# An eight-stage transformer stack on one core: stacked head operands issued inside later stages, a buffer of its own for head sums, sparse operands padded to 128 rows, and one first-layer operand made on ScalarE

## The chip, the core and the metric

The kernel runs on one core of a Trainium2 chip. The metric is device time in microseconds (us) of one execution. TensorE is called PE below, VectorE DVE, ScalarE ACT, GpSimd POOL, and SyncE (which only issues DMAs here) SP.

## The reference, cut to what matters

`x` is (1, 2048, 128), float32. Eight blocks follow each other, each added to `x` after a layernorm:

```
x = x + L0_attn(ln(x))   # windowed "bond" attention, 16 heads of 8, window 64
x = x + L0_ffn(ln(x));  x = x + L1_attn(ln(x));  x = x + L1_ffn(ln(x))
x = x + L2_attn(ln(x))   # dense attention fused with a top-k sparse attention
x = x + L2_ffn(ln(x));  x = x + L3_attn(ln(x));  x = x + L3_ffn(ln(x))
```

The parts that the change touches:

```
# L0_attn, for each head, query t and each of the 64 keys before it
strain = disp_win - disp
damage = sigmoid(gelu(strain @ W_dmg + b_dmg) @ W_dmg_out + b_dmg_out)
logits = gelu(strain @ W_strain + rel_emb @ W_pos) @ W_bond - 10 * damage

# L2_attn: 16 heads of 8, s = 2048, R = 64, kk = 409
dense  = softmax(q k^T / sqrt(8)) v  @ out_proj + b          # per head
QK     = (src Qp + bq) @ (src Kp + bk)^T / sqrt(64)           # 2048 x 2048, inner size 64
aw     = softmax(QK); keep the kk largest of each row, renormalise; sparse = aw @ V
x      = layernorm(src + sig(lam) * dense + (1 - sig(lam)) * sparse); ff; layernorm
# L3_attn: 16 heads of 8, plain softmax attention with scales
```

## The kernel before, in words

The kernel is written as a sequence of blocks. In a block each engine runs its own list; a block ends only when all five lists have ended (SP's too), and the next block starts then. Inside a block the order on an engine is the order in which the code issues, and waits are semaphores written by hand.

**First layer attention (`bond_attention`).** 256 tiles of 128x2048 are formed (a difference of a shifted window of `A` and the operand at t), put through Gelu on ACT (L630), and reduced by 32-column matmuls on PE (L453). They come in 8 phases of 32 tiles, each of 4 groups of 8 tiles. In a group, tiles 0 to 3 are made by POOL (L609) from an operand in SBUF, `l0a_a_of_t` (`atb`), and tiles 4 to 7 by DVE (L588, four pieces each) from one in PSUM. Each kind has a ring of 4 slots, so a maker waits until PE has reduced the tile 4 before it. `atb` of the next phase is made by DVE at offset 24 of 32 of the phase (`a_of_t_sbuf`, L491, a 128x512 subtraction from SBUF to SBUF). At offset 5 of phases 1 and 2 POOL also masks the first block of logits (L600), for which it waits for a copy that DVE makes at offset 13 of the same phase (L510).

**Heads of layers 2 and 3.** `head_prepare` projects q, k and v, splits q and k into three bf16 parts each, stores them in DRAM, computes a guard row, and then loads stacks: `Ks` (two slots, each 9 DMAs of 128 KB for 4 heads) and `Qs` (two query halves, each 9 DMAs of 64 KB and one of 24 KB from the guard). The products of parts are 75 rows deep. A head stage then runs segments of 64 turns: scores on PE (L1516), Exp on ACT (L1557), values on PE (L1530); DVE drains the sums at the segment's end, SP stores them and issues the stacks of a segment further on (`stack_next`). If the guard exceeds a bound (`over`), a maximum is computed in a branch; the profile shows no instruction of it.

**Layer 2 attention (`dual_attention`).** After `head_prepare` it runs two halves of 1024 queries. Each half has three blocks: (1) a sparse score block `l2q`: projections (L1846, L1850), their copies `l2q_k` and `l2q_q` of 64 rows, then 8 blocks of 128 queries: scores on PE (L1865), row maximum on DVE (L1890), Exp on ACT (L1878), over two PSUM sides, so PE may run two blocks ahead of ACT; (2) `l2x`: four head segments on PE and ACT beside the top-k search on DVE; (3) `l2v`: the values of the sparse part. The first half also stores the sparse V to DRAM (L1896) in block 1 and loads it in block 3 (L1994).

The lines that matter on SP at the end of block 2 of a half are:

```
hd.stack_next(sp, seg)                       # before the sums of the segment
...
sums_out(3)
sp.wait_ge(kept_o, 64 * (first + HSEG))      # until the sums have landed
```

`oT`, from which the sums are stored, belongs to block 2's own room in before, and the memory is given to others in block 3.

Of the kernel before, what the change touches and what calls it, by code (L numbers as in the profile page):

```python
# [5 lines left out]
P = 128  # L6
T = 2048
TB = T // P
# [161 lines left out]
def bond_attention(nc, g, I):  # L170
# [15 lines left out]
    with ExitStack() as ctx:  # L186
# [9 lines left out]
        hb = r.sb("half_bdo", [P, 1])  # L196
        V = r.sb("val", [P, TB, NH, HS + 1])
# [4 lines left out]
        with ExitStack() as ctx2:  # L202
# [68 lines left out]
            with nc.Block() as block:  # L271
# [17 lines left out]
                def _(dve):  # L289
# [10 lines left out]
                    dve.tensor_scalar(hb[:, :], bdo[:, :], 0.5, None, ALU.mult)  # L300
                    dve.wait_ge(pos_ps, 1)
# [50 lines left out]
        with nc.Block() as block:  # L352
# [109 lines left out]
            def _(dve):  # L462
# [16 lines left out]
                def a_of_t(p):  # L479
                    q, hf = divmod(p, 2)  # L480
                    at = slice(PAD + q * CH, PAD + (q + 1) * CH)
                    if p:
                        dve.wait_ge(diff_dve, len(D_AT) * GPP * p)
                    dve.tensor_copy(bank(1), A[:, hf, 1, at]).then_inc(at_ready, 1)

                def a_of_t_sbuf(p):
                    q, hf = divmod(p, 2)
# [3 lines left out]
                    dve.tensor_scalar(atb[:, p % 2, :], A[:, hf, 0, PAD + q * CH:PAD + (q + 1) * CH], bd[:, :], None,  # L491
                                      ALU.subtract).then_inc(atb_ready, 1)
# [54 lines left out]
                def tail(w, off):  # L547
# [14 lines left out]
                    if w + 1 < NPH and off == 24:  # L562
                        a_of_t_sbuf(w + 1)
# [8 lines left out]
                a_of_t_sbuf(0)  # L572
# [40 lines left out]
            def _(act):  # L613

                def exps(p):
                    act.wait_ge(emptied, use("l", p, LB - 1) + 1)
                    act.activation(E[:, :, :, :], E[:, :, :, :], ACT.Exp).then_inc(expd, 1)
                for s in range(NT):
# [633 lines left out]
def head_prepare(nc, g, ctx, tag, wqkv, bias, q_scale, k_scale):  # L1252
# [41 lines left out]
    hd.stack_next = stack_next  # L1294
    with ExitStack() as ctxg:
# [19 lines left out]
        with ExitStack() as ctx1:  # L1315
# [12 lines left out]
            with nc.Block() as block:  # L1328
# [87 lines left out]
                def _(sp):  # L1416
# [8 lines left out]
                    for i in range(2):  # L1425
                        sp.wait_ge(stored[i], 16 * 3 * NCH)
                    store_guard(sp, gsplit, gstored)
                    stack_k(sp, 0, 0, k_in[0])
                    stack_q(sp, 0, 0, q_in[0])
                    stack_q(sp, 0, 1, q_in[1])  # L1430
                    stack_k(sp, 1, 1, k_in[1])
                    sp.wait_ge(ones_in, 16)

        with ExitStack() as ctx2:
# [6 lines left out]
            with nc.Block() as block:  # L1441

                @block.tensor
                def _(pe):
                    flag = pe.value_load(over[0:1, 0:1], min_val=0, max_val=1)
                    with pe.If(flag > 0):
                        for k in range(2):
                            pe.wait_ge(q_in[k], QIN)
                            pe.wait_ge(k_in[k], KIN)
# [33 lines left out]
                def _(sp):  # L1483
                    flag = sp.value_load(over[0:1, 0:1], min_val=0, max_val=1)
                    with sp.If(flag > 0):
                        for k in range(2):
                            sp.wait_ge(q_in[k], QIN)
                            sp.wait_ge(k_in[k], KIN)
# [7 lines left out]
                        for qc in range(NQ):  # L1496
                            stack_q(sp, 0, qc, gstk)
                        stack_k(sp, 0, 0, gstk)
                        sp.wait_ge(gstk, GROUP * (G4 + 1) + 16 * NQ)
# [60 lines left out]
def head_attention(nc, g, tag, wqkv, bias, q_scale, k_scale, out_scale, OT):  # L1560


    with ExitStack() as ctx:
        hd = head_prepare(nc, g, ctx, tag, wqkv, bias, q_scale, k_scale)
# [9 lines left out]
        with nc.Block() as block:  # L1574
# [7 lines left out]
            def _(sp):  # L1582
                for seg in range(NSEG):
# [171 lines left out]
def dual_attention(nc, g, I):  # L1755
# [6 lines left out]
    with ExitStack() as ctx:  # L1762
# [5 lines left out]
        with ExitStack() as ctxh:  # L1768
# [30 lines left out]
            with nc.Block() as block:  # L1799
# [14 lines left out]

                @block.gpsimd
                def _(pool):
                    pool.wait_ge(brow, 1)
                    pool.tensor_tensor(dense[:, :, :], dense[:, :, :], rows[:, 0, :].unsqueeze(1).broadcast_to([P, TB, C]), ALU.add)
            hd = head_prepare(nc, g, ctxh, "l2m", w, (bqk[:, 0:1], bqk[:, 1:2], bv[:, :]), QS, 1.0)
# [7 lines left out]
            okr = rs.sb("row_ok", [P, 1])  # L1827
# [602 lines left out]
```

## Time and profile before

| | |
|---|---|
| median of 3 runs | 3283.6 us (3272.86 to 3292.04) |
| profiled execution | 3275.47 us, span 3273.8 us |
| busy, share of span | PE 2415.4 us (74%), DVE 2031.0 (62%), ACT 1973.0 (60%), POOL 971.7 (30%) |
| DMA | 144.67 MB, 44 GB/s over the span |
| mean granted PE clock | 0.882 of full speed |

The busy shares are means over stages that follow each other and have different limits. So the profile has to be read stage by stage: first attention from about 40 to 666 us, layer 2 attention from about 1468 to 2436 us, layer 3 attention from about 2615 us. The granted clock has two levels, 1.0 (2.4 GHz) and 0.5 (1.2 GHz); a stretch with a value between them has seen both.

### The profile page before, as it was taken

To read this page: it belongs to the slowest core of one execution; us is meant where nothing else is said; L and a number is where in the kernel's file an instruction comes from. 1 tells how busy PE (TensorE), PEld (TensorE's weight loads), DVE (VectorE), ACT (ScalarE), POOL (GpSimd) and SP (SyncE) were. 2 spreads that over 40 slices of the span, in tenths; PEclk is the share of its full clock that TensorE was granted. 3 is DMA by queue.
4 is the path that set the end of the run, shared out by engine and by line. 5 is a ranking of instruction groups with operands and counts; after the bars stand their busy time and mean duration, and the time that the engine had idled before them with its cause. 6 is when DMAs were issued, how large, how long until landed. Compare 5 with 4: busy or idle time off the path is not lost. (4 is left out here: it accounts for less than half of the span.)

```text
span 3273.8 us, 32822 instructions
## 1 busy us (share of the span) xinstructions
PE 2415.4 (74%) x12512; PEld 821.6 (25%) x12512; DVE 2031.0 (62%) x2781; ACT 1973.0 (60%) x1886; POOL 971.7 (30%) x358
## 2 busy tenths in 40 slices
PE   4567777675355555553799959999749839999995
PEld 1122222242111111321322223222434512222223
DVE  5888999677699999886289912899341250112115
ACT  4789999613433332212289943999532219999992
POOL 5889999420166666230000310003000000000000
PEclk8789999887699999986689976999969969999998
DMA  1011211200244443102201020000110030101000
GB/s 68 1 39 48 69 39 40 77 10 10 74 147 141 147 148 136 39 2 64 46 10 25 11 37 0 10 10 3 47 36 1 4 82 18 28 14 40 13 6 26
DMA packets 67031, 144.67 MB, mean 44 GB/s; under 512 B 15607, under 2 KB 30032, under 8 KB 66161
## 3 DMA queue, kind: packets, MB, share of 16 engines
q1 hardware_dynamic: 66864, 142.46, 15.2%
q8 instruction: 103, 1.69, 0.2%
q14 instruction: 64, 0.52, 0.1%
HBM read 117.99 MB, written 24.25 MB: 43 GB/s over the span
## 5 line engine op out<-in xcount | busy, mean ns | idle before, releaser
L609 POOL TENSOR_TENSOR l0a_diff_pool<-l0a_A,l0a_a_of_t 128x2048 f32<-128x2048 f32 x128 | 533.4, 4209 | 40.0 <-DVE l0a_a_of_t L491 34.3
L1557 ACT ACTIVATE l2x_pT<-ps 128x1024 f32<-128x1024 f32 x512 | 495.7, 1021 | 17.0 <-PE ps L1516 15.1
L1557 ACT ACTIVATE l3he_pT<-ps 128x1024 f32<-128x1024 f32 x512 | 496.0, 1021 | 4.1 <-PE ps L1516 2.2
L1032 PE MATMUL ps<-l1s_hc,all_ident 128*128 128x512 f32 x512 | 262.5, 639 | 250.7 <-DVE l1s_hc L1060 229.1
L1012 POOL TENSOR_TENSOR l1s_dBx<-l1a_dtx,l1s_Bs 128x1024 f32<-128x1024 f32 x128 | 301.1, 2353 | 291.1 <-DVE ps L1048 157.7
L588 DVE SCALAR_TENSOR_TENSOR l0a_diff_dve<-l0a_A,l0a_pos,ps 128x512 f32<-128x512 f32 x512 | 344.8, 741 | 29.1 <-PE ps L453 29.0
L1021 ACT ACTIVATE ps<-l1a_dt,l1a_A 128x1024 f32<-128x1024 f32 x128 | 143.0, 1118 | 321.6 <-DVE l1s_hc L1060 321.5
L1516 PE MATMUL ps<-l3h_Qs,l3h_Ks 75*128 75x512 bf16 x1024 | 267.8, 385 | 37.5 <-DVE ps L1604 37.5
L1974 POOL TENSOR_TENSOR l2s_E<-l2s_E,l2x_rest 128x2048 f32<-128x2048 f32 x16 | 72.7, 4546 | 735.7 <-DVEq L1704 730.6
L1619 DVE COPY l3he_oT<-ps 128x512 f32<-128x512 f32 x16 | 11.1, 692 | 445.1 <-PE ps L1530 445.0
L1516 PE MATMUL ps<-l2m_Qs,l2m_Ks 75*128 75x512 bf16 x1024 | 275.5, 394 | 9.8 <-PEq L1841 9.8
L1530 PE MATMUL ps<-l2x_pT,l2m_Va 128*9 128x512 f32 x2048 | 273.3, 607 | 1.2 <-ACT l2x_pT L1557 1.2
L630 ACT ACTIVATE l0a_diff_pool<-l0a_diff_pool 128x2048 f32<-128x2048 f32 x128 | 236.5, 1900 | 59.4 <-POOL l0a_diff_pool L609 59.3
L1530 PE MATMUL ps<-l3he_pT,l3h_Va 128*9 128x512 f32 x2048 | 268.4, 596 | 0.6 <-ACT l3he_pT L1557 0.6
L630 ACT ACTIVATE l0a_diff_dve<-l0a_diff_dve 128x2048 f32<-128x2048 f32 x128 | 237.8, 1899 | 15.3 <-DVE l0a_diff_dve L588 14.7
L453 PE MATMUL ps<-l0a_diff_pool,l0a_reducers 128*32 128x512 f32 x1024 | 157.4, 702 | 106.3 <-ACT l0a_diff_pool L630 105.2
L1665 DVE TENSOR_SCALAR_CACHE_REDUCE l2x_rest<-l2s_E,l2x_at 128x2048 f32<-128x2048 f32 x96 | 225.2, 2346 | 3.4
L453 PE MATMUL ps<-l0a_diff_dve,l0a_reducers 128*32 128x512 f32 x1024 | 153.6, 679 | 65.5 <-ACT l0a_diff_dve L630 64.4
L1032 PEld LDWEIGHTS ps<-l1s_hc,all_ident 128*128 128x128 f32 x512 | 90.9, 197 | 423.1 <-DVE l1s_hc L1060 329.7
L1516 PEld LDWEIGHTS ps<-l3h_Qs,l3h_Ks 75*128 75x128 bf16 x1024 | 79.8, 98 | 318.2 <-ACT l3he_pT L1557 218.9
L1060 DVE TENSOR_TENSOR l1s_hc<-ps,l1s_Cs 128x1024 f32<-128x1024 f32 x128 | 156.8, 1225 | 2.8 <-issue 0.6
L1516 PEld LDWEIGHTS ps<-l2m_Qs,l2m_Ks 75*128 75x128 bf16 x1024 | 81.2, 99 | 300.2 <-ACT l2x_pT L1557 222.5
(397 smaller groups left out, 3313.7 us busy)
## 6 DMA issues: line engine op xcount, KB each, us to landing
l1s_Bs<-l1a_bc SPq DMA_DIRECT2D x64, 512.0 KB, 3.6
l1s_Cs<-l1a_bc SPq DMA_DIRECT2D x64, 512.0 KB, 4.3
l0a_band_rows<-l0a_band SPq DMA_DIRECT2D x32, 512.0 KB, 5.7
l0a_band<-l0a_exps SPq DMA_DIRECT2D x16, 512.0 KB, 5.3
l2m_Ks<-l2m_parts SPq DMA_DIRECT2D x36, 128.0 KB
l2m_Qs<-l2m_parts SPq DMA_DIRECT2D x72, 64.0 KB
l3h_Ks<-l3h_parts SPq DMA_DIRECT2D x36, 128.0 KB
l3h_Qs<-l3h_parts SPq DMA_DIRECT2D x72, 64.0 KB
```

Source lines behind the costliest of these rows:

```text
L453: mm = pe.matmul(g.ps[32 * c:32 * c + 32, (2 + k) * CH:(3 + k) * CH], wbs[:, k, n, :], ge[:, c, :], start=(n == 0), stop=(n == 3))
L588: ins = dve.scalar_tensor_tensor(out[:, c, :], src[:, c, :], pos[:, d:d + 1], bank(1), ALU.add, ALU.subtract)
L609: pool.tensor_tensor(out, window(s), atb[:, p % 2, :].unsqueeze(1).broadcast_to([P, 4, CH]), ALU.subtract).then_inc(diff_pool, 1)
L630: act.activation(ge, ge, ACT.Gelu).then_inc(gelu_done, 1)
L1012: pool.tensor_tensor(db[:, m % NDB, :], dtx[:, i, h, half * TH:(half + 1) * TH], Bs[:, k % NBS, :], ALU.mult).then_inc(dbd, 1)
L1021: act.activation(hpair(m), dt[:, i, h, half * TH:(half + 1) * TH], ACT.Exp, scale=Al[:, i, h, n:n + 1]).then_inc(dad, 1)
L1032: mm = pe.matmul(g.ps[:, (4 + 2 * h + q) * CH:(5 + 2 * h + q) * CH], g.ident[:, :], hc[:, m % NHC, q * CH:(q + 1) * CH], start=(n == 0), s ...
L1060: dve.tensor_tensor(hc[:, m % NHC, :], hpair(m), Cs[:, k % NCS, :], ALU.mult).then_inc(hcd, 1)
L1516: mm = pe.matmul(g.ps[:, slot * QC + c * CH:slot * QC + (c + 1) * CH], hd.Ks[:, hg % 2, j, kt * P:(kt + 1) * P], hd.Qs[:, qc, j, c * CH:(c ...
L1530: mm = pe.matmul(g.ps[32 * j:32 * j + HS + 1, ACC + c * CH:ACC + (c + 1) * CH], hd.Va[:, kt, hg * 4 + j, :], pT[:, (4 * n + j) % NPT, c * ...
L1557: act.activation(pT[:, turn % NPT, :], g.ps[:, slot * QC:(slot + 1) * QC], ACT.Exp).then_inc(expd, 1)
L1665: step(dve.tensor_scalar(junk[:, b % 2, :], E[:, b, :], at[:, 0, b:b + 1], 0.0, ALU.is_ge, ALU.add, accum_out=at[:, 1, b:b + 1]))
```

## The change

- `bond_attention`: `a_of_t_sbuf` goes from DVE's list to ACT's (Identity with bias -b_dmg, a new column `nbd`). ACT makes it at offset 26 of a phase, the first one before its first tile. DVE's `a_of_t` gets a wait on `emptied`, which DVE itself counts.
- `head_prepare`: gets a parameter `early`. With `early` false (layer 2) no stack is issued in it; with true (layer 3) K stack 0 is issued ahead of the guard's store and Q stack 0 behind it, and the other two go to `stack_first` at the start of the head block. The branch for `over` is adapted.
- layer 2: all four first stacks are issued in the sparse score block of the first half, behind the V store. The stacks of segment 3 are issued in `l2v` of the first half, behind the V load. SP no longer waits at the end of `l2x` until the sums have landed; it does so in `l2v` of the second half ahead of loading them. `oT` belongs to the whole layer.
- layer 2: `l2q_q` and `l2q_k` have 128 rows, of which POOL sets 64 to 127 to zero; the score matmuls take all 128. POOL's addition of a bias row to `dense`, which had been in a block of its own engine list before `head_prepare`, follows these memsets in the first sparse block.

```diff
@@ bond_attention, DVE
 def a_of_t(p):
+    dve.wait_ge(emptied, use("a", q, 1, 1) + 1)
-def a_of_t_sbuf(p):
-    dve.wait_ge(emptied, use("a", q, 1, 1) + 1)
-    if p >= 2:
-        dve.wait_ge(diff_pool, (p - 1) * GPP * NP_)
-    dve.tensor_scalar(atb[:, p % 2, :], A[...], bd[:, :], None, ALU.subtract).then_inc(atb_ready, 1)
...
-                    if w + 1 < NPH and off == 24:
-                        a_of_t_sbuf(w + 1)
@@ bond_attention, ACT
+                a_of_t_sbuf(0)
                 for s in range(NT):
                     p, q, hf, dg, k, n = place(s)
+                    if p + 1 < NPH and s % TPP == 26:
+                        a_of_t_sbuf(p + 1)
@@ head_prepare, SP
                     for i in range(2):
                         sp.wait_ge(stored[i], 16 * 3 * NCH)
+                    if early:
+                        stack_k(sp, 0, 0, k_in[0])
                     store_guard(sp, gsplit, gstored)
-                    stack_k(sp, 0, 0, k_in[0])
-                    stack_q(sp, 0, 0, q_in[0])
-                    stack_q(sp, 0, 1, q_in[1])
-                    stack_k(sp, 1, 1, k_in[1])
+                    if early:
+                        stack_q(sp, 0, 0, q_in[0])
                     sp.wait_ge(ones_in, 16)
+    def stack_first(sp):
+        if not early:
+            stack_k(sp, 0, 0, k_in[0])
+            stack_q(sp, 0, 0, q_in[0])
+        stack_q(sp, 0, 1, q_in[1])
+        stack_k(sp, 1, 1, k_in[1])
@@ dual_attention, ahead of head_prepare
-                @block.gpsimd
-                def _(pool):
-                    pool.wait_ge(brow, 1)
-                    pool.tensor_tensor(dense[:, :, :], dense[:, :, :], rows[:, 0, :]..., ALU.add)
@@ dual_attention, l2q
-                    qs = r2.sb("q", [R, QC])
-                    ks = r2.sb("k", [R, T])
+                    qs = r2.sb("q", [P, QC])
+                    ks = r2.sb("k", [P, T])
+                            pool.memset(qs[R:P, :], 0.0).then_inc(zero, 1)
+                            pool.memset(ks[R:P, :], 0.0).then_inc(zero, 1)
+                            if half == 0:
+                                pool.wait_ge(zero, 2)
+                                pool.tensor_tensor(dense[:, :, :], dense[:, :, :], rows[:, 0, :]..., ALU.add)
@@ l2q, SP
                                 sp.dma_start(vdram, V[:, :, :]).then_inc(vst, 16)
+                                hd.stack_first(sp)
                                 sp.wait_ge(vst, 16)
@@ l2x, SP
-                                hd.stack_next(sp, seg)
+                                if i < HSEG - 1:
+                                    hd.stack_next(sp, seg)
-                            sp.wait_ge(kept_o, 64 * (first + HSEG))
@@ l2v, SP
                             sp.dma_start(V[:, :, :], vdram).then_inc(vin, 16)
+                            if half == 0:
+                                hd.stack_next(sp, HSEG - 1)
                             if half:
+                                sp.wait_ge(kept_o, 64 * NSEG)
```

On SP in layer 2, from the store of the guard to the end of the first sparse block, this stands before (the rows of the `over` branch, which stand between the two pieces, are left out):

```order
L1313 DMA l2m_mparts<-l2mg_guard_parts 16x2048 x3
L1274 DMA l2m_Ks<-l2m_parts 8x4x2048 x9
L1274 DMA l2m_Qs<-l2m_parts 8x4x1024 x9
L1281 DMA l2m_Qs<-l2m_mparts 3x4x1024
L1274 DMA l2m_Qs<-l2m_parts 8x4x1024 x9
L1281 DMA l2m_Qs<-l2m_mparts 3x4x1024
L1274 DMA l2m_Ks<-l2m_parts 8x4x2048 x9
...
L1892 UNCONDITIONAL_BRANCH
L1896 DMA l_sparse_values<-l2q_V 128x2048
L1841 UNCONDITIONAL_BRANCH
```

And this stands there in the changed kernel:

```order
L1324 DMA l2m_mparts<-l2mg_guard_parts 16x2048 x3
...
L1908 UNCONDITIONAL_BRANCH
L1912 DMA l_sparse_values<-l2q_V 128x2048
L1277 DMA l2m_Ks<-l2m_parts 8x4x2048 x9
L1277 DMA l2m_Qs<-l2m_parts 8x4x1024 x9
L1284 DMA l2m_Qs<-l2m_mparts 3x4x1024
L1277 DMA l2m_Qs<-l2m_parts 8x4x1024 x9
L1284 DMA l2m_Qs<-l2m_mparts 3x4x1024
L1277 DMA l2m_Ks<-l2m_parts 8x4x2048 x9
L1848 UNCONDITIONAL_BRANCH
```

The 38 DMAs of the stacks have moved from the end of the preparing block to behind the V store.

On ACT in the first attention, at offsets 16 to 31 of the first phase, the changed kernel has these rows; before, the first two rows with `l0a_diff_pool` and x2 were one row with x4 and nothing between them:

```order
L633 ACTIVATE l0a_diff_dve<-l0a_diff_dve 128x2048 x2
L633 ACTIVATE l0a_diff_pool<-l0a_diff_pool 128x2048 x2
L616 ACTIVATE l0a_a_of_t<-l0a_A,l0a_minus_bd 128x512
L633 ACTIVATE l0a_diff_pool<-l0a_diff_pool 128x2048 x2
L633 ACTIVATE l0a_diff_dve<-l0a_diff_dve 128x2048 x2
```

The operand that POOL needs for the next phase now stands between ACT's tiles 25 and 26, where DVE had it ahead of its tile 28.

On SP in layer 3, in the preparing block, the changed kernel has:

```order
L1435 DMA l3h_parts<-l3hp_pt 128x512 x24
L1277 DMA l3h_Ks<-l3h_parts 8x4x2048 x9
L1324 DMA l3h_mparts<-l3hg_guard_parts 16x2048 x3
L1277 DMA l3h_Qs<-l3h_parts 8x4x1024 x9
L1284 DMA l3h_Qs<-l3h_mparts 3x4x1024
```

Before, the three guard stores came first and all four stacks, 38 DMAs, followed; the remaining 19 now open the head block's list.

## Rows read from the trace of the kernel before

**Rows 1.** Timeline of DVE, first attention: start, us, instruction, [idle before <-releaser].

```profile
94.14 13.98 DVE L491 TENSOR_SCALAR l0a_a_of_t<-l0a_A,l0a_bd 128x512 f32<-128x512 f32 x1
```

**Rows 2.** Groups by line, 40 to 665 us: count | busy, mean ns | idle before.

```profile
L609 POOL TENSOR_TENSOR l0a_diff_pool<-l0a_A,l0a_a_of_t 128x2048 f32<-128x2048 f32 x128 | 533.4, 4209 | 40.0 <-DVE l0a_a_of_t L491 34.3 <-PE ps L453 5.7
...
L491 DVE TENSOR_SCALAR l0a_a_of_t<-l0a_A,l0a_bd 128x512 f32<-128x512 f32 x8 | 45.7, 5707 | 0.0
...
L627 ACT ACTIVATE l0a_tanh<-ps,l0a_half_bdo 128x512 f32<-128x512 f32 x32 | 21.4, 668 | 0.0
```

**Rows 3.** Timeline of ACT, end of phase 0 of the first attention.

```profile
112.28 1.91 ACT L630 ACTIVATE l0a_diff_dve<-l0a_diff_dve 128x2048 f32<-128x2048 f32 x1 [2.50 <-DVE l0a_diff_dve L588]
```

**Rows 4.** Timeline of POOL, first attention, the two masked phases.

```profile
140.36 1.09 POOL L600 TENSOR_SCALAR_AFFINE_SELECT l0a_exps<-l0a_exps 128x512 f32<-128x512 f32 x1 [15.56 <-DVE l0a_exps L510]
...
221.55 1.08 POOL L600 TENSOR_SCALAR_AFFINE_SELECT l0a_exps<-l0a_exps 128x512 f32<-128x512 f32 x1 [13.17 <-DVE l0a_exps L510]
```

**Rows 5.** ACT's waits from 222 to 626 us: total, times, longest.

```profile
ACT l0a_diff_dve L630 <- DVE l0a_diff_dve L588: 10.2, 10, 2.0
```

**Rows 6.** Timeline, layer 2 ahead of `head_prepare`.

```profile
1484.82 4.49 POOL L1818 TENSOR_TENSOR l2a_dense<-l2a_dense,l2a_rows 128x2048 f32<-128x2048 f32 x1 [14.64 <-DVEq L1799]
```

**Rows 7.** Timeline, end of the preparing block of layer 2.

```profile
1539.36 3.04 SPq L1274 DMA_DIRECT2D l2m_Ks<-l2m_parts  x9
...
1555.48 8.78 SPq L1274 DMA_DIRECT2D l2m_Ks<-l2m_parts  x9
...
1569.59 6.56 PE L1846 MATMUL ps<-all_hT,l2h_wp 128*64 128x512 f32 x8 [42.24 <-PEq L1441]
```

**Rows 8.** Timeline, first sparse score block.

```profile
1581.97 7.13 PE L1865 MATMUL ps<-l2q_k,l2q_q 64*128 64x512 f32 x16
...
1584.40 0.36 SPq L1896 DMA_DIRECT2D l_sparse_values<-l2q_V  x1
...
1590.15 38.95 PE L1865 MATMUL ps<-l2q_k,l2q_q 64*128 64x512 f32 x48 [1.04 <-ACT l2s_E L1878]
```

**Rows 9.** Windows, L1865 alone: us, busy (x) of PE, of its weight loads, clock, DMA share, GB/s.

```profile
1582.00:1592.50 10.50, 9.46 (x22) 4.03 (x23) 1.00 0.41 137
1592.50:1629.00 36.50, 36.50 (x44) 13.78 (x42) 0.50 0.00 0
1990.20:2043.50 53.30, 53.26 (x64) 20.50 (x64) 0.52 0.00 0
```

**Rows 10.** Windows: us, busy (x) of PE, PEld, DVE, ACT, POOL, then clock, DMA, GB/s.

```profile
1416.00:1462.00 46.00, 37.43 (x95) 15.52 (x96) 42.45 (x28) 4.56 (x16) 21.12 (x39) 1.00 0.00 1
1634.00:1661.00 27.00, 27.00 (x86) 4.82 (x87) 25.66 (x71) 15.98 (x17) 0.00 (x0) 0.50 0.00 1
1661.00:1690.00 29.00, 29.00 (x181) 6.41 (x180) 27.89 (x44) 28.54 (x31) 0.00 (x0) 1.00 0.00 1
```

**Rows 11.** Windows, same columns, while the first stacks of layer 2 land.

```profile
1585.00:1590.00 5.00, 4.11 (x10) 1.50 (x8) 3.15 (x2) 1.96 (x2) 0.00 (x0) 1.00 0.58 225
1590.00:1595.00 5.00, 4.85 (x9) 2.14 (x10) 1.44 (x1) 2.15 (x4) 0.00 (x0) 0.76 0.00 0
```

**Rows 12.** Timeline, ends of `l2x` in the first half (two rows) and the second.

```profile
1900.73 1.35 SPq L1932 DMA_DIRECT2D l2m_sums<-l2x_oT  x4
...
1924.61 1.94 PE L2012 MATMUL ps<-all_ident,l2s_E 128*128 128x128 f32 x8 [28.47 <-PEq L1912]
...
2306.33 1.94 PE L2012 MATMUL ps<-all_ident,l2s_E 128*128 128x128 f32 x8 [4.42 <-PEq L1912]
```

**Rows 13.** Timeline, end of the preparing block of layer 3.

```profile
2639.65 14.89 SPq L1424 DMA_DIRECT2D l3h_parts<-l3hp_pt  x14
...
2669.11 3.02 SPq L1274 DMA_DIRECT2D l3h_Ks<-l3h_parts  x9
...
2681.99 5.98 SPq L1274 DMA_DIRECT2D l3h_Ks<-l3h_parts  x9
...
2694.61 5.30 PE L1516 MATMUL ps<-l3h_Qs,l3h_Ks 75*128 75x512 bf16 x12 [37.46 <-DVE ps L1604]
```

More of the change, by code:

```diff
@@ L196, in bond_attention @@
         hb = r.sb("half_bdo", [P, 1])
+        nbd = r.sb("minus_bd", [P, 1])
         V = r.sb("val", [P, TB, NH, HS + 1])
@@ L617, in exps, with a_of_t_sbuf @@
                     act.activation(E[:, :, :, :], E[:, :, :, :], ACT.Exp).then_inc(expd, 1)
+                def a_of_t_sbuf(p):
+                    q, hf = divmod(p, 2)
+                    act.wait_ge(emptied, use("a", q, 1, 1) + 1)
+                    if p >= 2:
+                        act.wait_ge(diff_pool, (p - 1) * GPP * NP_)
+                    act.activation(atb[:, p % 2, :], A[:, hf, 0, PAD + q * CH:PAD + (q + 1) * CH], ACT.Identity,
+                                   bias=nbd[:, :]).then_inc(atb_ready, 1)
+                a_of_t_sbuf(0)
                 for s in range(NT):
                     p, q, hf, dg, k, n = place(s)
+                    if p + 1 < NPH and s % TPP == 26:
+                        a_of_t_sbuf(p + 1)
                     if s % TPP == 18 and p >= 1:
@@ L1249, with head_prepare @@
 HB = TB // 2
-def head_prepare(nc, g, ctx, tag, wqkv, bias, q_scale, k_scale):
+def head_prepare(nc, g, ctx, tag, wqkv, bias, q_scale, k_scale, early):
     BOUND = 40.0
@@ L1485, in _ @@
                     with sp.If(flag > 0):
-                        for k in range(2):
-                            sp.wait_ge(q_in[k], QIN)
-                            sp.wait_ge(k_in[k], KIN)
+                        if early:
+                            sp.wait_ge(q_in[0], QIN)
+                            sp.wait_ge(k_in[0], KIN)
                         for hg in range(G4):
@@ L1495, in _ @@
                         store_guard(sp, split, mst)
[L1496 to L1499, printed above, removed]
+                        sp.wait_ge(gstk, GROUP * G4)
+                        if early:
+                            stack_q(sp, 0, 0, gstk)
+                            stack_k(sp, 0, 0, gstk)
+                            sp.wait_ge(gstk, GROUP * G4 + QIN + KIN)
     return hd
@@ L1563, in head_attention @@
     with ExitStack() as ctx:
-        hd = head_prepare(nc, g, ctx, tag, wqkv, bias, q_scale, k_scale)
+        hd = head_prepare(nc, g, ctx, tag, wqkv, bias, q_scale, k_scale, True)
         sums = hd.sums
@@ L1813, in _ @@
                     act.activation(sc[:, :], lam[:, :], ACT.Sigmoid).then_inc(sig, 1)
-                @block.gpsimd
-                def _(pool):
-                    pool.wait_ge(brow, 1)
-                    pool.tensor_tensor(dense[:, :, :], dense[:, :, :], rows[:, 0, :].unsqueeze(1).broadcast_to([P, TB, C]), ALU.add)
-            hd = head_prepare(nc, g, ctxh, "l2m", w, (bqk[:, 0:1], bqk[:, 1:2], bv[:, :]), QS, 1.0)
+            hd = head_prepare(nc, g, ctxh, "l2m", w, (bqk[:, 0:1], bqk[:, 1:2], bv[:, :]), QS, 1.0, False)
             rs = Room(nc, ctxh, "l2s")
@@ L1841, in dual_attention, with _ @@
                     with nc.Block() as block:
+                        @block.gpsimd
+                        def _(pool):
+                            pool.memset(qs[R:P, :], 0.0).then_inc(zero, 1)
+                            pool.memset(ks[R:P, :], 0.0).then_inc(zero, 1)
+                            if half == 0:
+                                pool.wait_ge(zero, 2)
+                                pool.tensor_tensor(dense[:, :, :], dense[:, :, :], rows[:, 0, :].unsqueeze(1).broadcast_to([P, TB, C]), ALU.add)
                         @block.tensor
```

19 lines of the change are left out of this document (8 added, 11 removed).

## The prediction

> **What bounds the kernel now.** The chain that ended last covers 1% of the span, so it says nothing of where the time lies. I went by stages: first the page's slices to find them, then timelines of the engines at the places that the change touches, then windows for the granted clock.
>
> First attention: POOL makes 16 tiles of 4.2 us in each of 8 phases, some 67 us [rows 2]; outside two waits it hardly stands still, so POOL sets the pace. DVE's operand for it, L491, is a 128x512 operation, which should be short; one of them took 13.98 us [rows 1], and the eight took 45.7 us together [rows 2]. It is stretched while POOL is at work; the long one ended just when POOL had finished its phase, and afterwards ACT had waited 2.50 us for DVE's next tile [rows 3].
>
> Layer 2: three things show. (a) After the guard is stored SP issues 38 stack DMAs, from 1539.36 to 1564.26 us, in a block that can't end before; PE sits idle 42 us and begins 5.3 us after SP's end [rows 7]. (b) The sparse scores run at clock 1.0 for 10.5 us and then at 0.5 for 36.5 us, with PE busy all the time; in the second half nearly the whole 53.3 us are at 0.5 [rows 9]. At 1.0 two blocks take 8.18 us (1581.97 to 1590.15), and PE then waits 1.04 us for ACT [rows 8]; at 0.5 PE alone bounds, 8 pieces of 0.83 us a block. (c) At the end of `l2x` PE is idle 28.47 us in the first half and 4.42 us in the second [rows 12]. The difference is the stacks of segment 3: in the first half they are issued ahead of the sums, and SP waits until these have landed behind them.
>
> Layer 3: the same issue as (a), from 2669.11 to 2687.97 us, and PE starts 6.6 us behind its end [rows 13].
>
> **The change part by part.**
>
> *First attention.* The wait at POOL's first mask was 15.56 us and at the second 13.17 us [rows 4]. The second phase had no long L491 just ahead, so I take its wait as what the chain ACT, PE, DVE, POOL needs, and the first falls to it: -2.4 us. In the later phases POOL waited for PE 5.7 us in all [rows 2], ACT for DVE 10.2 us [rows 5], part of it behind long L491s. Against that ACT gets seven more operations inside the phases; the trace has none of this shape from SBUF, the nearest is the Tanh over 128x512, 0.67 us [rows 2], so 4.7 us if nothing covered them. ACT has the waits for POOL and DVE to cover them with. I take -2 us for the later phases, together -4.4; bounds -8.1 (2.4 and 5.7) and +4.7. The operation stands ahead of ACT's tile 26, and POOL can't begin the next phase before tile 24 is reduced, so POOL loses little by it. Behind it in ACT's list wait only the Gelus of tiles 26 and on. The new column and the first operand, ahead of a first tile that waits for POOL anyway, cost under 1 us.
>
> *The bias row on `dense`*: 4.49 us in a block that all others wait for [rows 6]. It goes behind two memsets on a POOL that is idle in the sparse block: -4.5. The memsets (64x1024 and 64x2048, about 3 us by the 4.49 us of a 128x2048 operation as the upper end each) have 12.4 us between the block's first projection and its first score [rows 7, 8]; without that cover they would cost what lies beyond.
>
> *Stacks out of layer 2's preparation.* SP's list ends at about 1539.4 instead of 1564.3; DVE's last work there ends at about the same time: -24.9. Issued behind the V store instead, they need again 24.9 us of issue in a block that will last some 33 us from there on, so they fit.
>
> *128-row operands.* The columns and so the pieces are the same, only the clock can change. At the higher clock a half takes three steps of 8.18 us and the last two blocks' 7.13 us [rows 8], 31.7 us. Before it was 47.1 us (1581.97 to 1629.10) and 53.3 us [rows 8, 9]: -15.4 and -21.6, together -37.0. Why the clock should stay up: the 64-row products fell to 0.5 with no pause at all, while the stretch from 1416 us, whose main products (L1189) have 128 rows, kept 1.0 with PE busy only 37.4 of 46 us [rows 9, 10]. What I can't see is whether rows of zeros count as rows. Bounds: 0 and -37.0; I take -37.0, since both stretches differ first in the number of rows used.
>
> The Trainium skill, "TensorE: Matmul & The Clock Gate", section "What's actually happening", says that the gate is set by how busy the PE has been recently, and its section on LDWEIGHTS that the row count doesn't matter to timing. By that a PE busy for all of 36.5 us would be at full clock, which the trace contradicts; if rows are not what lowers it, the padding gives nothing, and the sum would be 3204 us in place of 3167.
>
> *End of `l2x`.* The first half falls to the second's 4.42 us: -24.1. In both, SP no longer waits for the sums to land; of that I count 1 us each, as V's load then queues behind the sums and PE waits for V next: -2. The 19 DMAs behind V's load are issued in some 6 us of a block of about 55 us. Waiting for the sums ahead of `OT`'s load is hidden, as `OT` is used only at the block's end.
>
> *Layer 3.* The parts' last store is issued at 2654.5 us; with 2 us to land, K stack 0 can go at 2656.8, in SP's idle time. The four first stacks of layer 2 landed from 1539.4 until 1590 [rows 7, 11], 51 us; K stack 0 is a third of their bytes, so 17 us, until 2674. The guard's three stores were issued about 3 us ahead of 2669.11 and may stand behind it: SP is free between 2669.1 and 2674, I take 2672.5, plus 3.4 us for Q stack 0: 2675.9 instead of 2687.97, -12. Bounds: -15.5 (nothing waits) and -8 (all waits and Q stack 0, 8.5 us, lands late). Its remaining two stacks are needed one segment, about 60 us, later.
>
> **Sum:** 4.4 + 4.5 + 24.9 + 37.0 + 24.1 + 2 + 12 = 108.9 us. Against the profiled execution's own 3275.5 us that is 3166.6 us. The median of the three runs is 8 us above that execution, within their own spread of 19 us; I put the forecast slightly above the sum, at 3168 us.
>
> **The rivals.**
>
> 1. *Rows of zeros don't hold the clock* (0.12). For it: no row of before shows operands half of zeros. Against it: the identity is such an operand in the transposes, and those of `l2v` run in stretches at 1.0. The sparse blocks stay PE-bound and the 37.0 us are missing: about 3205 us.
>
> 2. *The first head stage waits for its stacks* (0.08). In the changed kernel the stacks start 14.8 us behind the block's first projection (1584.40 against 1569.59) [rows 7, 8], and the head stage starts 12.4 + 31.7 + 4.9 = 49 us behind it. The first K and Q stack are half of the 51 us, 25.5, and have V's 1 MB ahead of them, some 5 us: they land at about 45 to 47. The cover is 2 to 4 us. If the four stacks share the engines rather than follow each other, all land at 71, and 22 us are lost: 3190 us. It turns up as idle PE ahead of the first L1516.
>
> 3. *The head stages start at the other level of the clock* (inside the forecast's own range). After the first sparse block they ran 27 us at 0.5, with 86 pieces where 29 us at 1.0 held 181 [rows 10]. A step of 12 pieces takes 1.9 us at 1.0 and 1.85 us more at 0.5, so those 7 steps cost 13 us. A start at 1.0 would give up to 13 us: 3155 us; a longer stretch takes as much.
>
> 4. *Slower than before* (0.01): the same place, but the lower clock holds on through a half of layer 2. 109 / 1.85 = 59 steps of the 128 of the two halves would eat all that is won, against the 7 of before; for one full half, 64 steps or 118 us, it would be 3286 us. New alignments of PE's pauses could do it; no head stage of before stayed low for over 27 us.
>
> 5. *ACT becomes the bound of the first attention* (inside the range): -4.4 becomes +4.7, 3177 us.
>
> **How the numbers follow.** The forecast with rivals 3 and 5 as its spread has 0.75, rival 1 0.12, rival 2 0.08, rival 4 0.01, and 0.04 go to several parts falling short together (3210 to 3270). The likeliest case's own range is 3152 to 3186 us. The range for 8 in 10 is 3150 to 3207 us: it takes in rival 1 and rival 2 and leaves out some 1 in 10. A measurement of this kernel can tell about 0.5%, 16 us, from no change; every case but rival 4 and a corner of the last lies well below 3267. So faster 0.97, same 0.02, slower 0.01.
>
> **What would show it.** In the changed profile: L1846's idle time near 17 us instead of 42; L1865 in both halves in windows of clock 1.0 and about 32 us long each; the same, with ACT instead of PE as what is waited for; idle ahead of L1516 still 4.9 us (more is rival 2); idle PE ahead of the first transposes of `l2v` 3 to 4 us in both halves; PE's first L1516 of layer 3 about 12 us nearer to the parts' last store; no L491 on DVE and POOL's first mask wait near 13 us. The prediction is wrong above all if the second sparse block still takes over 50 us, or if a head stage stays at 0.5 for more than a few tens of us.

## The result, and the profile after

The changed kernel took 3160.19 us (median of 4 runs, 3153.26 to 3164.48) beside 3278.23 us for the kernel before on the same chip: a ratio of 0.9633, 95% interval 0.9594 to 0.9672, so 3.7% faster. The forecast was 3168 us. The profiled execution took 3153.26 us, with a span of 3151.5 us and a mean granted clock of 0.908. Against the span of before, 3273.8 us, 122.3 us are gone. I split them by the time at which the same PE instruction starts in both traces:

| stretch | term of the prediction | between the profiles |
|---|---|---|
| first attention, to its last transposes of logits | -4.4 | -10.7 |
| from there to layer 2 (nothing changed) | 0 | +2.0 |
| bias row on `dense` | -4.5 | -4.6 |
| stacks out of layer 2's preparation | -24.9 | -25.1 |
| first sparse block, score to head stage | -15.4 | -15.6 |
| first head stage and its end | -24.1, -1 | -34.7 |
| second sparse block | -21.6 | -21.6 |
| second head stage and its end | -1 | -2.4 |
| preparation of layer 3 | -12 | -11.3 |
| all the rest | 0 | +1.7 |

**First attention** ([rows 1 to 5]). Groups by line, 40 to 655 us:

```profile
L601 POOL TENSOR_TENSOR l0a_diff_pool<-l0a_A,l0a_a_of_t 128x2048 f32<-128x2048 f32 x128 | 532.4, 4211 | 34.7 <-ACT l0a_a_of_t L616 34.7
...
L616 ACT ACTIVATE l0a_a_of_t<-l0a_A,l0a_minus_bd 128x512 f32<-128x512 f32 x7 | 5.0, 708 | 0.0
```

Timeline of POOL:

```profile
135.13 1.09 POOL L592 TENSOR_SCALAR_AFFINE_SELECT l0a_exps<-l0a_exps 128x512 f32<-128x512 f32 x1 [12.42 <-DVE l0a_exps L505]
...
335.71 66.49 POOL L601 TENSOR_TENSOR l0a_diff_pool<-l0a_A,l0a_a_of_t 128x2048 f32<-128x2048 f32 x16 [0.58 <-ACT l0a_a_of_t L616]
402.80 66.52 POOL L601 TENSOR_TENSOR l0a_diff_pool<-l0a_A,l0a_a_of_t 128x2048 f32<-128x2048 f32 x16 [0.60 <-ACT l0a_a_of_t L616]
```

ACT's operation takes 0.71 us every time (before, DVE's took 5.7 us on average). The first mask wait is 12.42 us instead of 15.56, and the later phases follow each other every 67.1 us, with waits of 0.6 us only.

**Layer 2** ([rows 6 to 12]). Timeline, from the preparing block to the first head stage:

```profile
1476.41 4.61 PE L1356 MATMUL ps<-all_hT,l2w_wqkv 128*128 128x512 f32 x5 [3.15 <-PEq L1809]
...
1531.28 5.92 PE L1861 MATMUL ps<-all_hT,l2h_wp 128*64 128x512 f32 x8 [17.06 <-PEq L1452]
...
1542.93 7.03 PE L1881 MATMUL ps<-l2q_k,l2q_q 128*128 128x512 f32 x16
1545.45 0.35 SPq L1912 DMA_DIRECT2D l_sparse_values<-l2q_V  x1
...
1579.37 5.28 PE L1525 MATMUL ps<-l2m_Qs,l2m_Ks 75*128 75x512 bf16 x12 [4.88 <-PEq L1848]
```

The idle time ahead of the sparse block has fallen from 42.24 to 17.06 us; the 4.88 us ahead of the head stage are the same as in before, so the head stage does not wait for its stacks (rival 2 did not happen). The clock of the two sparse blocks, windows of PE (us, busy (x), granted clock, DMA share, GB/s):

```profile
1542.93:1579.37 36.44, 28.44 (x67) 0.97 0.52 96
1902.16:1938.66 36.50, 28.50 (x64) 1.00 0.00 0
```

The ends of `l2x` and the wait for V behind the first:

```profile
1835.31 1.06 PE L2031 MATMUL ps<-all_ident,l2s_E 128*128 128x128 f32 x8 [2.72 <-PEq L1928]
...
1840.92 2.04 PE L2039 MATMUL ps<-l2v_pT,l2v_V 128*128 128x512 f32 x2 [4.55 <-DMA l2v_V<-l_sparse_values]
...
2194.18 1.47 PE L2031 MATMUL ps<-all_ident,l2s_E 128*128 128x128 f32 x8 [2.72 <-PEq L1928]
```

28.47 us have become 2.72, 25.7 less. The other 9 us of the first head stage are clock. Windows of the first 30 us of the head stages, the two of layer 2 and that of layer 3; a clock of 0.87 over 30 us means 8 us at 0.5 (30 x (1 - 0.87) x 2), where before had 27 [rows 10]:

```profile
1579.40:1609.40 30.00, 30.00 (x160) 0.87 0.22 39
1938.70:1968.70 30.00, 30.00 (x164) 0.89 0.00 1
2572.10:2602.10 30.00, 30.00 (x156) 0.86 0.25 58
```

**Layer 3** ([rows 13]). Timeline:

```profile
2544.90 3.04 SPq L1277 DMA_DIRECT2D l3h_Ks<-l3h_parts  x9
2554.57 1.24 SPq L1324 DMA_DIRECT2D l3h_mparts<-l3hg_guard_parts  x3
...
2561.41 3.97 SPq L1277 DMA_DIRECT2D l3h_Qs<-l3h_parts  x9
...
2572.06 5.30 PE L1525 MATMUL ps<-l3h_Qs,l3h_Ks 75*128 75x512 bf16 x12 [26.21 <-DVE ps L1614]
```

The guard's stores, issued at 2554.57, hold Q stack 0 back until 2561.41. The view of DMAs gives them a median of 5.5 us from issue to landing; in before it was 2.2 us. So the guard does stand behind K stack 0, as the prediction had it.

### The profile page after: what moved, and what is told of

It is laid out like the page before. It is cut to its first block and busy times, and to the rows that moved or that the text cites. A ratio compares the mean times of both kernels' runs of the same rounds, so it can differ in the third digit from the quotient of the medians.

```text
span 3151.5 us, 32834 instructions
## 1 busy us (share of the span) xinstructions
PE 2361.9 (75%) x12512; PEld 803.9 (26%) x12512; DVE 1985.7 (63%) x2774; ACT 1977.1 (63%) x1894; POOL 976.1 (31%) x362
## 5 line engine op out<-in xcount | busy, mean ns | idle before, releaser
L601 POOL TENSOR_TENSOR l0a_diff_pool<-l0a_A,l0a_a_of_t 128x2048 f32<-128x2048 f32 x128 | 532.4, 4211 | 34.7 <-ACT l0a_a_of_t L616 34.7
L633 ACT ACTIVATE l0a_diff_pool<-l0a_diff_pool 128x2048 f32<-128x2048 f32 x128 | 237.7, 1901 | 54.0 <-POOL l0a_diff_pool L601 53.9
```

What stands on the lines that cost most here:

```text
L601: pool.tensor_tensor(out, window(s), atb[:, p % 2, :].unsqueeze(1).broadcast_to([P, 4, CH]), ALU.subtract).then_inc(diff_pool, 1)
L633: act.activation(ge, ge, ACT.Gelu).then_inc(gelu_done, 1)
```

## The experiments

Each ran beside the kernel before on the same chip; "after" is the changed kernel. The ratio is to the kernel before, whose own median lay between 3266 and 3278 us beside them. The stages from layer 0's FFN to layer 1's, which no edit touches, took 800 to 810 us in the fourteen profiles. So medians that lie under some 10 us apart say little, and the stages of the traces are compared first.

**Operands of 64 rows again (e1_rows64).**

```diff
-                    qs = r2.sb("q", [P, QC])
-                    ks = r2.sb("k", [P, T])
+                    qs = r2.sb("q", [R, QC])
+                    ks = r2.sb("k", [R, T])
-                            pool.memset(qs[R:P, :], 0.0).then_inc(zero, 1)
-                            pool.memset(ks[R:P, :], 0.0).then_inc(zero, 1)
```

> The changed kernel, with the operands of the sparse scores back at 64 rows (POOL's two memsets go with them; its addition to dense stays). My theory: the rows decide TensorE's clock, so both sparse blocks fall back to 0.5 and take 47 and 53 us from first score on, in place of 31.7: +37 us. The head stage after each then starts at 0.5, for some 27 us in the first half instead of 10: up to +9 more. Total +37 to +46, about 3200 us. Rival: the clock stayed up because the stacks or something else in the block changed (SP's transfers beside it, another alignment), not because of the rows: both blocks stay at 1.0, total +0. A second rival: only the second half depends on the rows, +21.

Measured: 3203.95 us (3198.8 to 3206.64), ratio 0.9789 (0.9753 to 0.9826). The sparse blocks took 52.5 and 57.5 us from score to head stage, in place of 36.4 and 36.5: +16.1 and +21.0. Windows:

```profile
1558.00:1600.30 42.30, 37.42 (x44) 0.50 0.43 77
1924.00:1981.50 57.50, 52.57 (x65) 0.52 0.00 0
```

The rows decide. The miss: I had also expected the first head stage to start with some 27 us at 0.5, as in before, because the block ahead of it ended at 0.5. It had 9 us (clock 0.85 over its first 30 us), while the second head stage had 27 us. The level at which the block ahead ended is not what sets this: in e3 and e8 the second sparse block ran at 1.0, and the second head stage had 27 us at 0.5 all the same.

**Operands of 96 rows (e8_rows96).** `[P, ...]` becomes `[96, ...]`, with rows 64 to 95 zeroed.

> The changed kernel, with the operands of the sparse scores of 96 rows (32 of zeros in place of 64). It asks whether the clock follows the number of rows in steps or needs all 128. Theory A: 96 rows hold 1.0 in both blocks, +0 us. Theory B: they fall to 0.5 as 64 do, +37 us. Theory C: in between, with some stretches at 0.5, +5 to +30 us. I lean to A (0.5) over C (0.3).

Measured: 3167.76 us (3163.71 to 3171.93), ratio 0.9666 (0.9634 to 0.9698). Theory A held. The second block's window:

```profile
1901.90:1938.40 36.50, 28.50 (x64) 1.00 0.00 0
```

**The kernel before with the padding alone (e7_before_padded).**

> The kernel before, with the 128-row operands (memsets of the lower 64 rows on POOL) and nothing else of the change. If the edits are independent, the sparse blocks take 36.4 us each from first score to head stage: -15.6 and -21.6, so -37 us against the kernel before. Rival 1: there the stacks' transfers lie otherwise beside the block and the clock falls in spite of the rows: less than -20 us. Rival 2: in the one half or other the head stage starts 18 us longer at 0.5, which takes 9 us back: -28 us.

Measured: 3226.98 us (3221.14 to 3244.67), ratio 0.986 (0.9818 to 0.9903), about 46 us faster by the ratio, 54 us between the profiles. Its sparse blocks took 36.4 and 36.5 us: -15.6 and -21.6, as forecast. Most of the rest, 19 us, lies at two places in the first head stage that this edit does not touch, and that vary between executions: 7 us at 0.5 at its start in place of 27, and an end of the first `l2x` of 18.72 us in place of 28.47, with the same DMAs in the same order. Against that, the second head stage and the preparation of layer 3 were 5 us longer each.

```profile
1884.72 1.94 PE L2019 MATMUL ps<-all_ident,l2s_E 128*128 128x128 f32 x8 [18.72 <-PEq L1919]
```

**Stacks in the preparing block again (e6_stacks_in_preparation).**

```diff
                     if early:
                         stack_q(sp, 0, 0, q_in[0])
+                    else:
+                        stack_first(sp)
@@ l2q, SP
-                                hd.stack_first(sp)
```

> The changed kernel, with layer 2's four first stacks issued at the end of the preparing block again. My theory: SP's 24.9 us of issue stand in a block that can't end before, PE's first L1861 has 42 us of idle time ahead of it in place of 17: +25 us, and nothing is given back later, as the stacks weren't waited for in the changed kernel. Rival: the stacks land earlier for the head stage, and V's store and load find an emptier queue, which gives back part: +15 us or less.

Measured: 3191.57 us (3182.61 to 3192.52), ratio 0.9725 (0.9692 to 0.9759). The idle time ahead of the sparse block is back, +25.8 us, and nothing of it is given back: sparse block 36.4 us, head stage 255.5 (after: 255.9). The median is 31 us above after's; 7.7 us of the profile's difference are a longer second head stage, which this edit does not touch.

```profile
1564.71 5.12 PE L1863 MATMUL ps<-all_hT,l2h_wp 128*64 128x512 f32 x8 [42.86 <-PEq L1454]
```

**Segment 3's stacks ahead of the sums, no wait for landing (e5_stacks_ahead_of_sums).** In `sums_out` the condition `if i < HSEG - 1` goes, and so does `stack_next` in `l2v`.

> The changed kernel, with segment 3's stacks of the first half issued ahead of the sums again, inside l2x, but without the wait for the sums to land. It splits the 24 us of the end of l2x. Theory A, issue time: the sums and the row okrow go out 19 DMAs later (some 6 us), nothing waits for more, since the next block needs okrow's store and then V; idle PE between the head stage and l2v goes from 2.7 to 9 us, +6 us. Theory B, bytes: the stacks' transfers fill the engines and okrow's landing comes behind them, in spite of the missing wait: idle PE near 28 us, +24 us.

Measured: 3184.66 us (3174.57 to 3191.22), ratio 0.971 (0.9671 to 0.9748). Timeline:

```profile
1839.40 0.88 PE L2028 MATMUL ps<-all_ident,l2s_E 128*128 128x128 f32 x3 [6.55 <-PEq L1928]
...
1859.19 2.05 PE L2036 MATMUL ps<-l2v_pT,l2v_V 128*128 128x512 f32 x2 [17.85 <-DMA l2v_V<-l_sparse_values]
```

Neither theory held. The block's end is free of the stacks' bytes (6.55 us against 2.72), but V's load, issued behind them, is what waits now: 17.85 us against 4.55. The values of the first half start 18 us later than in after, measured at the next block's start too (1911.7 against 1893.7 us). SP had issued V's load at 1839.37 us, 4 us later than in after, and it landed 19.7 us after its issue, in after 5.5 us. So the stacks' bytes are the cost, and not the time that SP needs to issue them; the wait only decided which instruction paid it.

**The wait for landing alone (e4_landing_wait).** `sp.wait_ge(kept_o, 64 * (first + HSEG))` is back at the end of `l2x`.

> The changed kernel, with SP's wait for the sums to land at the end of l2x put back, and nothing else. The stacks are no longer ahead of the sums, so a landing costs only itself: idle PE between the head stage and l2v goes from 2.72 to 4.4 us, and V's load then finds an empty queue, so the wait for V falls from 4.55 towards 3.0: +0.2 to +1.8 us a half, +1 to +3.6 us in all (the prediction's term was 2). Rival: the wait was the cause of the 28 us by itself, +20 us or more in the first half.

Measured: 3172.97 us (3163.06 to 3175.76), ratio 0.9703 (0.9667 to 0.9738). Timeline:

```profile
1837.37 1.94 PE L2032 MATMUL ps<-all_ident,l2s_E 128*128 128x128 f32 x8 [5.24 <-PEq L1928]
...
1842.46 2.04 PE L2040 MATMUL ps<-l2v_pT,l2v_V 128*128 128x512 f32 x2 [3.15 <-DMA l2v_V<-l_sparse_values]
```

+2.5 us and -1.4 us, so 1.1 us in this half; in the second the end takes 4.38 us in place of 2.72. The rival is out. The median is 13 us above after's, more than the edit can be seen to cost; three of its four runs had a mean granted clock of 0.898 or 0.899, those of after 0.903 to 0.909. Why is open.

**The operand on DVE again (e2_operand_on_dve).** `a_of_t_sbuf` stands in DVE's list at offset 24, as before.

> The changed kernel, with GpSimd's operand made by DVE again (tensor_scalar between two SBUF tiles, as before the change). It measures the first attention's part alone. By the stage's last Exp in the two traces the part gave 10.7 us, so +10.7 us with DVE's operation again stretched to 14 us at its longest; by the prediction's term +4.4 us. Rival: the gain of the stage came from elsewhere (its waits fall otherwise in each run), 0.

Measured: 3174.44 us (3166.47 to 3185.41), ratio 0.9704 (0.9659 to 0.9748). The stage ended 19.7 us later than in after. The instruction by its line (count, then min/median/max in ns, first and last start):

```profile
L494 DVE TENSOR_SCALAR l0a_a_of_t<-l0a_A,l0a_bd x8: 486/12314/13970, 40.2 to 539.9; 128x512 f32<-128x512 f32 x8
```

Timeline of POOL, the second mask and a later phase:

```profile
223.75 1.08 POOL L602 TENSOR_SCALAR_AFFINE_SELECT l0a_exps<-l0a_exps 128x512 f32<-128x512 f32 x1 [15.88 <-DVE l0a_exps L512]
...
469.43 83.30 POOL L611 TENSOR_TENSOR l0a_diff_pool<-l0a_A,l0a_a_of_t 128x2048 f32<-128x2048 f32 x20 [4.28 <-PE ps L455]
```

In this execution more of the eight were stretched than in that of before, whose median was 2.6 us with nearly the same longest:

```profile
L491 DVE TENSOR_SCALAR l0a_a_of_t<-l0a_A,l0a_bd x8: 486/2598/13980, 40.9 to 531.0; 128x512 f32<-128x512 f32 x8
```

What the change removes is thus worth 10.7 us by one execution, 19.7 by another, and 7.1 by that of the kernel before with the padding alone (e7). It goes with the number of operations over 9 us: three of eight in before, five in e2, two in e7, so 3.6 to 3.9 us for each.

There is nothing between short and long. The first of the eight finds POOL at rest; the other 21 of these three profiles began beside a POOL tile. Eleven ended 0.3 us behind the end of that tile, 1.5 to 3.3 us after their start. The other ten ended only 0.3 us behind the last tile that POOL could make without this very operand, 9.7 to 14.0 us after their start: they lost every turn between two tiles and got through once POOL stopped for them. In before, L491 [rows 1] ended at 108.12 us; POOL's timeline around it:

```profile
91.18 16.66 POOL L609 TENSOR_TENSOR l0a_diff_pool<-l0a_A,l0a_a_of_t 128x2048 f32<-128x2048 f32 x4
108.19 8.33 POOL L609 TENSOR_TENSOR l0a_diff_pool<-l0a_A,l0a_a_of_t 128x2048 f32<-128x2048 f32 x2 [0.36 <-DVE l0a_a_of_t L491]
```

Which of the two happens stays open.

**On DVE, with a third operand in PSUM (e3_operand_on_dve_psum).**

```diff
-    act.activation(atb[:, p % 2, :], A[...], ACT.Identity, bias=nbd[:, :])
+    dve.scalar_tensor_tensor(atb[:, p % 2, :], A[...], bd[:, :], bank(1), ALU.subtract, ALU.bypass)
```

> The changed kernel, with GpSimd's operand made by DVE again, but by an operation that has a third operand in PSUM whose value does not enter (the same result). Theory A: DVE's form with both tensors in SBUF is what POOL's work stretches, one with a PSUM operand is not: each such operation takes about 0.7 us, and the time is that of the changed kernel, +0 to +2 us. Theory B: every DVE operation of this place waits, whatever its operands: as the kernel with tensor_scalar, +4 to +11 us, with single operations near 14 us.

Measured: 3162.78 us (3154.68 to 3166.76), ratio 0.9666 (0.9628 to 0.9705). Theory A held, with the stage 2.8 us shorter than in after. By line, and then a row of POOL's timeline:

```profile
L495 DVE SCALAR_TENSOR_TENSOR l0a_a_of_t<-l0a_A,l0a_bd,ps x8: 742/743/748, 39.1 to 521.9; 128x512 f32<-128x512 f32 x8
```

```profile
334.70 132.94 POOL L612 TENSOR_TENSOR l0a_diff_pool<-l0a_A,l0a_a_of_t 128x2048 f32<-128x2048 f32 x32 [0.20 <-PE ps L455]
```

The same engine at the same place is not stretched in this form. The edit changes the instruction together with adding an operand in PSUM, so which of the two frees it is not separated. The Trainium skill, "SBUF — State Buffer", section "SBUF: two separate sides", says that DVE (in a form that takes both ports) and GpSimd share one pair of ports under a lock, held for a whole instruction. The trace agrees on who is stretched, and in that each of the 21 operations counted in e2 ended just behind a POOL tile; the 13.97 us are over three POOL tiles of 4.2 us, so one lost turn does not explain them.

**Head operands of 128 rows (e9_head_rows128).** `Qs` and `Ks` get 128 partitions, POOL zeroes rows 64 to 127, and the row of ones is loaded after that.

> The changed kernel, with the operands of the heads' scores (Qs, Ks, 75 rows of bf16 in both layers) padded to 128 rows: POOL zeroes rows 64 to 127 early in the preparing block, and the row of ones is loaded after that. It asks whether the time at 0.5 at the start of each head stage (8, 7 to 27 and 22 us in the profiles so far) is a matter of rows too. Theory A, rows: the low stretches shrink to nothing, up to -4 us, -3 to -12 us and -10 us: -15 to -25 us. Theory B: the low stretch follows PE's pause of 5 us or more ahead of each head stage, whatever the operands: 0 us, with low stretches of the same lengths.

Measured: 3155.19 us (3152.96 to 3159.35), ratio 0.9639 (0.9587 to 0.969). Windows of the first 30 us of the three head stages:

```profile
1581.70:1611.70 30.00, 29.96 (x168) 0.93 0.24 41
1938.40:1968.40 30.00, 29.97 (x165) 0.90 0.00 1
2574.00:2604.00 30.00, 29.97 (x166) 0.91 0.43 59
```

4, 6 and 5 us at 0.5 (after: 8, 7 and 8): shorter, not gone. The edit also costs something: from PE's first instruction of layer 2 to the first sparse projection it took 58.0 us, in after 54.9. The start at 0.5 follows PE's pause, as theory B says, but its length is not quite independent of the rows.

**Layer 3's Q stack ahead of the last K parts (e10_queries_first).**

> The changed kernel, with layer 3's Q stack 0 read as soon as Q's parts have landed, in SP's idle time ahead of K's last stores, so that only its guard row is left behind the guard's landing. Q stack 0's nine issues (4.0 us in the changed kernel's trace) leave SP's end of the block, and the guard's stores no longer find K stack 0 alone in the queues ahead of them: PE's first L1525 of layer 3 comes 4 to 5 us earlier after the last transposed kmax: -4 us. Rival: K's parts are stored later by the nine issues ahead of them, and K stack 0 with the guard behind it too: 0 to +2 us.

Measured: 3159.68 us (3156.43 to 3169.93), ratio 0.9654 (0.9599 to 0.9708). No gain; PE's first L1528 of layer 3 comes 29.9 us behind the last transposed kmax (after: 26.4). The guard's landing has become the wait, 13.4 us from issue by the view of DMAs, and SP issues the guard row of Q at 2573.72 (timeline):

```profile
l3h_mparts<-l3hg_guard_parts SPq DMA_DIRECT2D x3, 64.0 KB, 13.4
```

```profile
2573.72 0.25 SPq L1445 DMA_DIRECT2D l3h_Qs<-l3h_mparts  x1
```

The rival came true, and more: what is saved in issue time goes to bytes ahead of the guard.

**GpSimd's mask later (e11_mask_at_11).** `s % TPP == 5` becomes `s % TPP == 11`.

> The changed kernel, with GpSimd's mask in the first attention after three more of its tiles (at offset 11 of the phase in place of 5), in the two phases that have one. POOL stood still 12.4 and 13.4 us there for DVE's copy, and can do three tiles of 4.2 us in that time. Theory A, POOL sets the pace of this stage: the two waits all but vanish, -20 to -25 us, if DVE, which then waits for the mask, catches up within the phase. Theory B: DVE is bound by its own tiles behind the mask in these phases and carries the wait on to PE and POOL: -5 us or less.

Measured: 3151.25 us (3143.77 to 3157.11), ratio 0.9621 (0.9568 to 0.9675). Timeline of POOL:

```profile
136.19 1.09 POOL L592 TENSOR_SCALAR_AFFINE_SELECT l0a_exps<-l0a_exps 128x512 f32<-128x512 f32 x1 [0.35 <-DVE l0a_exps L505]
162.22 45.36 POOL L601 TENSOR_TENSOR l0a_diff_pool<-l0a_A,l0a_a_of_t 128x2048 f32<-128x2048 f32 x11 [3.38 <-PE ps L455]
208.86 1.08 POOL L592 TENSOR_SCALAR_AFFINE_SELECT l0a_exps<-l0a_exps 128x512 f32<-128x512 f32 x1 [1.27 <-DVE l0a_exps L505]
251.39 49.91 POOL L601 TENSOR_TENSOR l0a_diff_pool<-l0a_A,l0a_a_of_t 128x2048 f32<-128x2048 f32 x12 [3.34 <-ACT l0a_a_of_t L616]
```

Both waits are nearly gone, some 3 us of each come back behind them, and the stage is 16.6 us shorter: most of theory A. Of that, 7 us were lost again before layer 2 began, in stages which this edit does not touch, and 6 us in a longer start at 0.5 of the second head stage, in the profiled execution.

**Three edits together (e12_combined).** The operand as in e3, the mask as in e11, the heads' rows as in e9.

> The changed kernel with three edits of earlier runs together: the operand for GpSimd made by DVE with a third operand in PSUM (there all its operations took 0.74 us), the mask after three more tiles (the stage was 17 us shorter), and the heads' operands padded to 128 rows (1 to 3 us). By their stages -3, -17 and -2 us, some of which may be given back in the second layer's scan, whose length varied by 5 us between profiles: 3135 to 3145 us against the changed kernel's 3160, a ratio of 0.957 to 0.960 to the kernel before. Rival: DVE, which waits for the mask and now has the operand too, falls behind in the first three phases, and the combination is no faster than the mask's edit alone, 3150 us.

Measured: 3141.2 us (median of 6 runs, 3132.58 to 3144.08), ratio 0.9599 (0.9572 to 0.9625), in the forecast stretch: about 19 us under after's median; the profiled execution is 13 us under after's. The stage of the first attention ended 17.7 us earlier than in after, and the second head stage started with a clock of 0.94 over its first 30 us.

## Why the prediction was right, point by point

- *Rows hold the clock*: shown. 64 rows cost 16.1 and 21.0 us (e1), 64 rows of zeros behind them give back just that, also on the kernel before (e7: 15.6 and 21.6), and 32 rows of zeros do as well (e8). Rival 1 is out: the rule of the Trainium skill that was weighed there ("TensorE: Matmul & The Clock Gate", "What's actually happening"), read as the engine's busy time alone, fails here, since with 64 rows PE was busy without a pause, 37.42 us up to the 4.88 us ahead of the head stage, at clock 0.50, and with 128 rows 28.5 us of 36.5 at 1.00. What that page says of the row count, which the prediction put beside it, is about the time of a weight load, not about the clock.
- *Stacks out of the preparation*: shown, 25.8 us (e6). The cover was enough: 4.88 us ahead of the head stage in all kernels.
- *Bias row*: -4.6 us, read from the traces only; no run undid it.
- *End of `l2x`*: the size was right, the reason half. I had put the 24 us down to SP waiting behind the stacks for the sums. With that wait gone and the stacks still ahead, 18 us remain (e5), now as a wait for V; the wait alone costs 1 to 2 us a half (e4). What helped is that the stacks stand behind V's load. The size held some luck: the same end took 18.72 us in e7, whose code is that of before there, and by that profile the term would have been some 14 us.
- *Layer 3*: the mechanism was right, -11.3 against -12; no run undid it by itself. The guard behind K stack 0 landed 5.3 to 10.4 us after its issue in the profiles of kernels that share this order (before: 2.2), so the term varies: the start behind the last transposed kmax was 26.4 to 31.1 us, against 37.6 (before) and 42.7 (e7) in the old order.
- *First attention*: the term was mis-sized, -10.7 against -4.4. The part on the masks held: from the start of one POOL phase to the next, the first with a mask went from 83.5 to 80.7 us (-2.4 forecast), the second stayed (81.2 and 81.8); where a long operation stood ahead of the second mask too, in e2, its wait was 15.88 us. The step that failed is "I take -2 us for the later phases", and the bound of 5.7 us that went with it: phases 4, 5 and 7 (counted from 0) took 68.8, 68.7 and 68.4 us before and 67.1, 67.1 and 66.5 after, some 5 us, and 1.7 us more went behind POOL's last tile, a place which the sum left out. Another 1.7 us stand ahead of POOL's first tile, which began at 41.5 us in before and 39.8 in after; e1, with after's code there, began at 41.1 and e7, with before's, at 39.8, so they are not the edit's. And the whole depends on the execution, since which operations are stretched changes: 7, 11 and 20 us (e7, before and e2, against after). ACT did not become the bound (rival 5): its waits are for POOL, 53.9 us in all.
- *Start of the head stages* (rival 3, counted at nothing): -9 us in the first half. No single part of the change is behind it: all twelve experiments had 4 to 9 us at 0.5 there, e1 (64 rows) and e7 (nothing but the padding) too. Whether before's 27 us are the rule for that kernel, one profile can't tell; it stays open. The second head stage had 7 to 27 us at 0.5 in kernels that don't differ there, for 255.5 to 264.9 us of length. After's profiled execution had a short start at both places, which may be part of the 7 us that it lies under the median; but of after's other three runs one had a mean clock as high, 0.909, and took 3159.07 us, so it is not shown.

The first attention's -6.3 us and the head stage's -9 us beyond the forecast, 3.7 us lost in stages that did not change, and under 2 us of small differences lead from the sum, 3166.6, to the profile's 3153.3; the median of the runs, 3160.2, lies between.

## What to carry to other kernels

Before taking a wait out, ask whose bytes lie in the queue behind it: they find the next waiter, as V's load did here. A matmul that is PE-bound with half of the rows empty is worth padding with zeros when the profile shows it busy at clock 0.5. And where GpSimd works all the time, give a DVE operation between SBUF tiles to ACT, or let it read an operand from PSUM, and judge it by several executions, since which instructions are stretched changes.

## What the runs showed of the hardware

- Matmuls of 128x512 f32 with 64 rows: the granted clock fell to 0.5 with PE busy throughout (37.42 us of e1 at 0.50). With 96 or 128 rows, 32 or 64 of them zeros, it stayed at 1.0 with PE busy 28.5 of 36.5 us.
- The start of a head stage behind 4.88 us of idle PE ran at 0.5 for 7 to 27 us with operands of 75 rows and the same instructions, PE busy all the time. Windows of the second head stage, from e3 and then from e12 (heads' operands of 128 rows):

```profile
1939.10:1969.10 30.00, 29.98 (x105) 0.55 0.00 1
```

```profile
1928.10:1958.10 30.00, 29.38 (x168) 0.94 0.00 1
```

With 128 rows it was 3 and 6 us in the two profiles that there are, against 7 to 8 us in three and 12 to 27 in nine with 75. Over all three head stages, the six starts with 128 rows (e9, e12) had 3 to 6 us at 0.5, and the 36 with 75 rows 7 to 27. No start of the one kind reaches the other, so the rows seem to shorten it; but it rests on two executions.
- A 128x512 subtraction on DVE from SBUF to SBUF took 0.49 us with GpSimd at rest and 1.49 to 13.98 us beside its work, ending just behind a GpSimd tile in all 21 cases: either the one in which it began, or the last before GpSimd stopped for it. The form with an operand in PSUM took 0.74 to 0.75 us in all eight cases of e3 and as much in e12.
- Stores of 64 KB landed 2.2 us after their issue where they stood ahead of the stacks (before), 5.3 to 10.4 us behind 1.1 MB of loads from the same queue (layer 3's guard), and a 1 MB load 19.7 us after its issue behind 1.8 MB, in place of 5.5 (e5 against after).
